# Attended sums from fp32r high and low parts, group parts by pairs of tiles, an update in 64x64 pieces

## The reference

```python
h = tok_ref(x)                      # embeddings, layer norm, 8 heads of 64: Q, V; erase and update of traces; V_ret @ W_out.T
h = h + attn_ref(layernorm(h))      # below
h = h + ffn_ref(layernorm(h))       # soft mixture of 64 experts, 16 slots each

def attn_ref(x):
    q, k, v = split(x @ W_qkv + b_qkv)
    gw = softmax(gelu(v @ W_gp))                     # 49 groups
    group_weight = gw @ gw.T
    attn = softmax((q @ k.T) * scale * group_weight)
    a = sigmoid(alpha)
    return (((1 - a) * attn + a * group_weight) @ v) @ W_proj + b_proj
```

## Time and profile before

| | before |
|---|---|
| median of 3 runs | 452.79 us (452.72 to 452.94) |
| profiled execution | 452.15 us, of which the traced span is 450.3 us |
| granted PE clock | 1.00 of full speed (2.4 GHz) in every slice |
| the chain that ended last | PE 73%, DMA 9%, DVE 7%, POOL 5% of the span |
| PE busy | 427.2 us (95%); DVE 294.2 (65%), ACT 229.5 (51%), POOL 138.8 (31%) |
| costliest group | L918, 256 instructions, 46.2 us |

### The profile page before, as it was taken

The page is one execution under the profiler, slowest core; times in us unless marked ns, Lnnn a source line. Parts: engine busy times, 40 slices in busy tenths (PEclk is TensorE's granted clock), DMA queues, the critical chain, the costliest instruction groups (busy, mean ns, idle before and its releaser), DMA issues.

```text
span 450.3 us, 8295 instructions
## 1 busy us (share of the span) xinstructions
PE 427.2 (95%) x3098; PEld 355.3 (79%) x3098; DVE 294.2 (65%) x755; ACT 229.5 (51%) x415; POOL 138.8 (31%) x233
## 2 busy tenths in 40 slices
PE   7899999999999999899999999999999799999995
PEld 5667757788888887788888888899965477787895
DVE  6689773885857577777775777767775253454464
ACT  5587734798624636643324557978864312112220
POOL 5875110673100019500002780013731421211310
PEclk9999999999999999999999999999999999999999
DMA  3226100301000000500000000006359999999404
GB/s 99 65 66 223 61 2 0 106 2 29 1 1 1 0 1 0 212 1 1 0 0 1 2 0 1 1 1 270 152 208 408 378 352 381 390 366 382 143 12 140
DMA packets 14231, 50.23 MB, mean 112 GB/s; under 512 B 3504, under 2 KB 8240, under 8 KB 9968
## 3 DMA queue, kind: packets, MB, share of 16 engines
q1 hardware_dynamic: 7584, 43.21, 25.7%
q0 software_dynamic: 2912, 3.96, 3.1%
q10 hardware_dynamic: 3696, 2.54, 1.8%
HBM read 46.53 MB, written 3.15 MB: 110 GB/s over the span
## 4 chain that ended last, share of the span: by engine, by line
PE 73%; DMA 9%; DVE 7%; POOL 5%; issue 2%; ACT 2%; SPq 0%; POOLq 0%; DVEq 0%
DMA w1r<-in_p_w 9%; PE ps L918 8%; PE ps L964 8%; PE ps L1120 7%; PE ps L1061 3%; PE ps L898 2%; PE ps L692 2%; PE ps L1090 2%; PE ps L1107 2%; PE ps L944 2%; PE ps L596 2%; PE ps L945 2%; PE ps L947 2%; PE ps L948 2%; PE ps L946 2%
## 5 line engine op out<-in xcount | busy, mean ns | idle before, releaser
L918 PE MATMUL ps<-pr,et 128*128 128x192 f32 x256 | 46.2, 331 | 1.7 <-DVE et L1777 1.2
L1120 PE MATMUL ps<-ys,ct 128*128 128x192 f32 x256 | 45.2, 330 | 1.4 <-DMA ys<-ys_dram 1.4
L1952 DVE TENSOR_TENSOR res<-ps,res 128x384 f32<-128x384 f32 x64 | 35.7, 558 | 14.9 <-PE ps L1120 10.4
L1120 PEld LDWEIGHTS ps<-ys,ct 128*128 128x128 f32 x256 | 41.2, 190 | 4.8 <-issue 2.7
L918 PEld LDWEIGHTS ps<-pr,et 128*128 128x128 f32 x256 | 41.2, 189 | 4.5 <-ACT et L1348 2.7
L584 POOL DMA_DIRECT2D ys<-ys_dram x32 | 19.6, 617 | 69.8 <-DMA ys_dram<-ysb 68.9
L1464 ACT ACTIVATE hs<-ps 128x384 f32<-128x384 f32 x16 | 7.8, 490 | 58.5 <-PE ps L1061 58.5
L500 POOL TENSOR_SCALAR ve<-mv 128x1 f32<-128x1 f32 x32 | 10.0, 312 | 75.1 <-DVE mv L1792 41.9
L1337 ACT ACTIVATE scs<-ps,pr 128x1024 f32<-128x1024 f32 x16 | 17.8, 1114 | 29.9 <-PE ps L866 29.9
L1341 ACT ACTIVATE zz<-zz,nmx 128x1024 f32<-128x1024 f32 x16 | 18.4, 1151 | 26.0 <-DVE nmx L1771 25.8
L1943 DVE COPY ysb<-ps 128x192 f32<-128x192 f32 x16 | 5.7, 357 | 39.4 <-PE ps L1090 39.4
(11 more groups left out here) (314 smaller groups left out, 1175.4 us busy)
## 6 DMA issues: line engine op xcount, KB each, us to landing
w1r<-in_p_w SPq DMA_DIRECT2D x16, 1152.0 KB, 19.7
w2r<-in_p_w SPq DMA_DIRECT2D x16, 1152.0 KB, 19.3
ys_dram<-ysb ACTq DMA_DIRECT2D x16, 96.0 KB, 8.7
ys<-ys_dram POOLq DMA_DIRECT2D x32, 48.0 KB, 7.2
phT<-in_p_phi SPq DMA_DIRECT2D x1, 1024.0 KB, 4.8
wT<-in_p_qkv SPq DMA_DIRECT2D x1, 774.0 KB
out<-res SPq DMA_DIRECT2D x3, 192.0 KB, 3.4
out<-res ACTq DMA_DIRECT2D x3, 192.0 KB, 3.8
```

Source lines behind the costliest of these rows:

```text
L918: last = mm(d[:, 0:D], et[:, k, :], pr[:, b * KT + k, 1:1 + D], start=(k == 0), stop=(k == KT - 1))
L1120: last = mm(bank(5 + q % 3)[:, h * D:(h + 1) * D], ct[:, u % 2, k + h, :], ys[:, t % YR, b, :], start=True, stop=True)
L1952: v.tensor_tensor(res[:, i:i + 2, :], bank(5 + q % 3)[:, 0:2 * D].rearrange("p (h d) -> p h d", h=2), res[:, i:i + 2, :], ALU.add).then_in ...
```

## The change

- `attend(i)` no longer multiplies plain fp32. The exponentials are turned as before, but ACT now copies both halves into `et` as fp32r, and DVE subtracts (PSUM bank minus `et`) into a new tile `etl`, half by half, each half behind ACT's. POOL splits the values once per batch into `V[b]`: 192 columns hi, 192 columns lo. PE makes 8 fp32r products of `et` with all 384 columns of `V`, then 8 of `etl` with the 192 hi columns. DVE's `finish` adds both column blocks with the weight `cn`.
- The group part leaves `attend`: `u_pair(p)` makes it for two tiles at once (4 fp32r products) into bank 7, behind `turn(s-1)` in odd steps, and DVE adds 384 columns in one operation (`u_add`). On DVE `weight` moves from before `turn` to behind `z_tile`.
- POOL runs `values_hi(0)` before the first clearing of `X1L`, `values_lo(0)` right behind it, `values_hi(1)` and `values_lo(1)` behind the second clearing.
- SP loads ring buffer 0 only after all attended sums (`o_filled` = 16), because `V1` lies there.
- The update makes eight 64x64 pieces (16 products, M = 64, N = 64), which ACT copies at once.
- In the front, `hi_parts(0)` comes one step earlier on ACT, `masked` moves ahead of `normalise`, four warming products on PE come one step earlier, and DVE's copy of `wpT`'s row and the `eyeP` scalings move from behind tile 13 to step 2.
- `scores` is split in two functions; the order of its instructions stays.

```diff
         scs = sb("scs", [P, S], where=late)
-        et = sb("et", [P, KT, P], where=late)
+        et = sb("et", [P, KT, P], F32R, late)
...
         phT = sb("phT", [P, 2, NS], where=params)
+        etl = sb("etl", [P, KT, P], F32R, params)
+        V = [sb("V0", [P, KT, 2 * D], F32R, params)]
...
         KV = XC + W2N
+        tables = ExitStack()
+        V.append(sb("V1", [P, KT, 2 * D], F32R, tables))
+        tables.close()
...
+        U_PAIRS = NT // 2
+        def u_sums_at(b):
+            return 2 * b + 1
+        def u_pair_at(p):
+            return 3 + p if p else 2
...
             return acc_bank(b, j).rearrange("p (t c) -> p t c", c=256)
+        def half_turned(t, half):
+            return t[:, half * (KT // 2):(half + 1) * (KT // 2), :].rearrange("p k c -> p (k c)")
...
             sp.wait_ge(m["bias_ready"], 1)
+            sp.wait_ge(m["o_filled"], NT)
...
             pool.wait_ge(m["half_ready"], 1)
+            def values_hi(b):
+                nc.gpsimd.tensor_copy(V[b][:, :, 0:D], pr[:, b * KT:(b + 1) * KT, 1:1 + D]).then_inc(m["v_split"], 1)
+            def values_lo(b):
+                if b:
+                    pool.wait_ge(m["v_split"], 2 * b + 1)
+                nc.gpsimd.tensor_tensor(V[b][:, :, D:2 * D], pr[:, b * KT:(b + 1) * KT, 1:1 + D],
+                                        V[b][:, :, 0:D].bitcast(F32), ALU.subtract).then_inc(m["v_split"], 1)
+            pool.wait_ge(m["pr_taken"], KT)
+            pool.wait_ge(m["h_filled"], NT)
+            pool.wait_ge(m["h_taken"], NT)
+            values_hi(0)
+            pool.wait_ge(m["v_split"], 1)
...
                 nc.gpsimd.memset(X1L[b][DB:P, 1, :].bitcast(F32), 0.0).then_inc(m["x1l_zeroed"], 1)
+                if b == 0:
+                    pool.wait_ge(m["x1l_zeroed"], 1)
+                    values_lo(0)
+                    pool.wait_ge(m["v_split"], 2)
...
             pool.wait_ge(m["ones_written"], 1)
+            pool.wait_ge(m["pr_taken"], NT)
+            values_hi(1)
+            values_lo(1)
...
                     tok_T(s - 1)
-                if s == 2:
+                if s == 1:
...
             pe.wait_ge(m["bs_ready"], 2)
-            for t in range(HP):
-                c = slice(t * P, (t + 1) * P)
-                mm(bank(5)[:, c], wvT[:, 0, c], bs[:, 0, c], start=True, stop=False)
-                last = mm(bank(5)[:, c], wvT[0:DB, 1, c], bs[0:DB, 1, c], start=False, stop=True)
+            for h in range(HEADS):
+                t, r = divmod(h, 2)
+                c = slice(h * DT, (h + 1) * DT)
+                d = bank(5)[r * DT:(r + 1) * DT, t * DT:(t + 1) * DT]
+                mm(d, wvT[:, 0, c], bs[:, 0, c], start=True, stop=False)
+                last = mm(d, wvT[0:DB, 1, c], bs[0:DB, 1, c], start=False, stop=True)
...
                 if b:
-                    pe.wait_ge(m["et_copied_v"] if r else m["et_copied_a"], 2 + r)
+                    pe.wait_ge(m["et_copied_v"], 6 if r else 3)
...
                 pe.wait_ge(m["qpl_taken"], 2 * QPS - 2 + b)
+                if b:
+                    pe.wait_ge(m["u_taken"], u_pair_at(0))
...
-            def scores(i, held):
+            def query_keys(i, held):
...
                 last.then_inc(m["s_filled"], 1)
-                if i == 0:
-                    for j in range(QPS + 2, 2 * QPS):
-                        query(j)
+            def group_scores(i, held):
+                b, k = divmod(i, KT)
+                n = slice(k * P, (k + 1) * P)
...
                 if i >= 1:
-                    pe.wait_ge(m["et_copied_a"], i)
-                    pe.wait_ge(m["et_copied_v"], i)
+                    pe.wait_ge(m["et_copied_v"], 2 * i)
...
                 b, k = divmod(i, KT)
-                n = slice(k * P, (k + 1) * P)
+                if k == 0:
+                    pe.wait_ge(m["v_split"], 2 * (b + 1))
...
                     pe.wait_ge(m["o_taken"], i - 1)
-                else:
-                    pe.wait_ge(m["u_taken"], i + 1)
+                if i == 0:
+                    pe.wait_ge(m["u_taken"], u_sums_at(0))
+                elif i == 1:
+                    pe.wait_ge(m["u_taken"], u_sums_at(1))
+                elif i % 2:
+                    pe.wait_ge(m["u_taken"], u_pair_at(i // 2))
                 d = bank(6 + i % 2)
-                mm(d[:, 256:256 + D], gD[b][:, n], uP[:, b, :], start=True, stop=False)
-                mm(d[:, 256:256 + D], gL[b][:, n], uP[:, b, :], start=False, stop=True)
-                for k in range(KT):
-                    if k == 0:
-                        pe.wait_ge(m["et_copied_a"], i + 1)
-                    if k == KT // 2:
-                        pe.wait_ge(m["et_copied_v"], i + 1)
-                    last = mm(d[:, 0:D], et[:, k, :], pr[:, b * KT + k, 1:1 + D], start=(k == 0), stop=(k == KT - 1))
+                for c in range(KT):
+                    if c % (KT // 2) == 0:
+                        pe.wait_ge(m["et_copied_a"], 2 * i + 1 + c // (KT // 2))
+                    mm(d[:, 0:2 * D], et[:, c, :], V[b][:, c, :], start=(c == 0), stop=False, skip_group_check=True)
+                for c in range(KT):
+                    if c % (KT // 2) == 0:
+                        pe.wait_ge(m["et_copied_v"], 2 * i + 1 + c // (KT // 2))
+                    last = mm(d[:, 0:D], etl[:, c, :], V[b][:, c, 0:D], start=False, stop=(c == KT - 1), skip_group_check=True)
                 last.then_inc(m["o_filled"], 1)
+            def u_pair(p):
+                pe.wait_ge(m["u_taken"], u_sums_at(1) if p else u_sums_at(0))
+                if p:
+                    pe.wait_ge(m["o_taken"], 2 * p)
+                for h in range(2):
+                    b, k = divmod(2 * p + h, KT)
+                    n = slice(k * P, (k + 1) * P)
+                    d = bank(7)[:, h * D:(h + 1) * D]
+                    mm(d, gD[b][:, n], uP[:, b, :], start=True, stop=False)
+                    last = mm(d, gL[b][:, n], uP[:, b, :], start=False, stop=True)
+                last.then_inc(m["u_filled"], 1)
...
                 if s < NT:
-                    scores(s, pass_tiles(s - 1))
+                    query_keys(s, pass_tiles(s - 1))
+                if s == 0:
+                    for j in range(QPS + 2, 2 * QPS):
+                        query(j)
+                if s < NT:
+                    group_scores(s, pass_tiles(s - 1))
...
                     turn(s - 1)
+                if s % 2:
+                    u_pair(s // 2)
...
             for s in range(NT + 3):
-                if 2 <= s < NT + 2:
+                if s == 1:
+                    hi_parts(0)
+                if 3 <= s < NT + 2:
                     hi_parts(s - 2)
+                if 2 <= s <= NT:
+                    masked(s - 2)
...
                     masked_q(s - 3)
-                if 2 <= s <= NT:
-                    masked(s - 2)
...
             act.wait_ge(m["update_done"], 1)
-            for r in range(2):
-                rows = slice(r * DT, (r + 1) * DT)
-                last = sc.copy(tt[rows, :, :], bank(5)[rows, :].rearrange("p (t c) -> p t c", t=HP)[:, :, r * DT:(r + 1) * DT])
-            last.then_inc(m["update_taken"], 1)
+            sc.copy(tt[:], bank(5)[:, 0:HP * DT].rearrange("p (t c) -> p t c", t=HP)).then_inc(m["update_taken"], 1)
...
                     act.wait_ge(m["in_phi"], 16 * 4)
-                    act.wait_ge(m["u_filled"], NB)
+                    act.wait_ge(m["u_filled"], u_sums_at(1))
...
             def turn(i):
-                act.wait_ge(m["et_filled"], 2 * i + 1)
...
                     act.wait_ge(m["o_filled"], i)
-                sc.copy(et[:, 0:KT // 2, :].rearrange("p k c -> p (k c)"), bank(4)).then_inc(m["et_copied_a"], 1)
+                for half in range(2):
+                    act.wait_ge(m["et_filled"], 2 * i + 1 + half)
+                    sc.copy(half_turned(et, half), bank(4 + half)).then_inc(m["et_copied_a"], 1)
...
                     lo_parts(s - 2)
+                if s == 2:
+                    v.tensor_copy(wpT[DB:DB + 1, 1, :], beta_row).then_inc(m["setup_taken"], 1)
+                    for r in range(2):
+                        rows = slice(r * DT, (r + 1) * DT)
+                        v.tensor_scalar(eyeP[rows, :], ident[rows, rows], TRACE_DECAY, None, ALU.mult)
...
                     wrap(0)
-                if s == NT + 1:
-                    v.tensor_copy(wpT[DB:DB + 1, 1, :], beta_row).then_inc(m["setup_taken"], 1)
-                    for r in range(2):
-                        rows = slice(r * DT, (r + 1) * DT)
-                        v.tensor_scalar(eyeP[rows, :], ident[rows, rows], TRACE_DECAY, None, ALU.mult)
...
                 d = bank(6 + b)[:, 0:D]
-                dve.wait_ge(m["u_filled"], b + 1)
+                dve.wait_ge(m["u_filled"], u_sums_at(b))
...
                                        ALU.subtract).then_inc(m["u_taken"], 1)
+            def u_add(p):
+                dve.wait_ge(m["u_filled"], u_pair_at(p))
```

(16 more changed lines are left out.)

2 lines of the change are left out of this document (1 added, 1 removed).

## The result

| | before | changed |
|---|---|---|
| median | 452.87 us (4 runs, 452.72 to 453.21) | 457.26 us (4 runs, 456.02 to 460.65) |
| ratio | | 1.0107, 95% interval 1.0086 to 1.0127 |
| profiled execution | 452.15 us, span 450.3 | 456.25 us, span 454.5 |
| mean granted clock of the 4 runs | 1.00 in the profiled one | 0.996, 0.988, 0.982, 0.990 |

The kernel became slower by 1.1%. The direction was the likeliest in the prediction, the size was not: 454.3 was forecast, with a range that ended at 456.8. And the runs now lie 4.6 us apart, the longest with the lowest clock.

The account below looks back on a forecast made before the run. PE, busy 95% at full clock, was taken as the bound, with POOL and DVE in its way in attention. Front -3.7, turns 0, collisions +3.3 and +1.9 gave +1.5 on 452.15: 453.65, median 454.3 (+0.64); range 449.3 to 456.8.

Parts of the forecast that it names:

- loop of the front: Front, PE-bound loop: with masked ahead, PE's waits for xm go and the loop starts earlier, -1.5 us.
- `cc`: Front: DVE's row copy and scalings leave the way of cc, for which PE waited 1.09; -1.0 us.
- update in pieces: Front: 16 products of 64x64 pieces take 2.1 us in place of 3.33; -1.2 us.
- first collision: Batch 0, before gw_T: POOL's values_lo(0) holds the shared port against DVE's L1667; PE +3.3 us.
- second collision: Before the first sum: values_lo(1) on POOL holds up DVE's small L1729, delaying uP; +1.9 us (0 to 2.5).
- group products ahead of tile 0's sum, four for two: Attention: 4 products of 0.11 in every second gap of 1.28 between transposes and sum, taken as free.
- turns, tile 0 to 15: Attention loop: new sums save PE 0.28 per turn, 4.5 over 16 turns, but DVE and ACT waits leave zero.
- Tile 1: Attention: its sum waited for uP and then two products, now only for uP; -0.3 us.
- Tiles 4 to 8: Attention, steps 5 to 8: DVE's side work delays remainders and ACT; +1.4 us, lag +1.1 at tile 8.
- Tile 15: Last attention turn: its transposes wait for exps, which comes 0.9 later within the turn; +0.7 us.
- the locks don't bite: Rival on POOL's splits: DVE wins the port or the small operation passes; 449.1 us, chance 0.26 shared with PE's gain whole.
- slower still: Rival in the attention loop: remainders come too late in every turn, 16 x 0.2 lost, 457.5 us; chance 0.10.

Follow-up runs that it names:

- e2: Changed kernel with POOL's values_lo(0) and values_lo(1) each waiting until DVE has written that batch's group weights; 452.67 us median, ratio 0.9996.
- e3: e2 with the update in four 128x128 blocks as in the kernel before; 450.01 us median, ratio 0.9936.
- e6: e5 plus twelve products nobody reads in PE's idle stretch ahead of the transposed group weights; 453.99 us, ratio 1.0025.
- e8: Kernel before with the reordered front alone, old update and old attended sums; 449.37 us median, ratio 0.9916.
- e5: Changed kernel with the old update in four 128x128 blocks, both POOL-DVE collisions left in; 455.53 us, ratio 1.0049.
- e1: Changed kernel with only POOL's values_lo(0) waiting for DVE's group weights of batch 0; 454.63 us median, ratio 1.0033.
- e13: e3 with DVE's side work spread, z_tile ahead of turn, and values_lo(1) also waiting for the bias tables' remainders; 444.44 us, ratio 0.9876.
- e7: Kernel before with the update in eight 64x64 pieces and ACT's single copy, nothing else; 453.98 us median, ratio 1.0028.
- e4: Changed kernel, collisions left in, plus twelve products nobody reads in PE's idle 3 us ahead of the transposed group weights; 458.22 us median.
- e9: e3 with DVE's side work (reduction, scalings, remainders) and ACT's two casts spread over other steps; 446.89 us, ratio 0.9915.
- e11: e3 with z_tile moved ahead of turn on DVE; 448.86 us, ratio 0.9957.
- e15: e2 with one 512-column fp32r product nobody reads behind each of the eight update pieces; 455.17 us median, ratio 1.0088.

## Why the prediction was wrong, step by step

The prediction's sum was +1.5 against the profiled execution; measured is +4.1 (456.25 against 452.15). Two steps carry the miss: the update, put at -1.2, and the clock, for which the sum has no term. Term by term:

| step | predicted | measured | from |
|---|---|---|---|
| loop of the front | -1.5 | -1.6 | 2.66 at L670 less the wait for `cc` |
| `cc` | -1.0 | -1.1 | the wait of 1.09 is gone |
| update in pieces | -1.2 | +0.45 | e2 against e3 |
| first collision | +3.3 | +2.84 | `gw_T` at 113.15 against 112.58 - 2.26 |
| second collision | +1.9 | +1.2 | e6 against e3 at tile 0, 4.04, less 2.84 |
| group products ahead of tile 0's sum, four for two | 0 | +0.2 | e3 against e8 at tile 0 |
| clock behind the stall | none | +1.4 | the rest at tile 0; 1.54 in e5 against e6 |
| turns, tile 0 to 15 | 0 | +0.5 | table |
| tile 15 to the end | 0 | +0.2 | span +4.2 |

**Right: both collisions.** Their place, their order and the operations they hit were as put down, and e1, e2 and e13 show that the operation is back at 0.57, 0.16 and 0.76 once the split stands elsewhere. The page SBUF — State Buffer of the Trainium skill (Who interferes with whom) says that issue order decides who blocks, and that a DVE instruction with two SBUF inputs collides with a GpSimd instruction that reads SBUF; the runs agree three times, down to an operation of a single column. The sizes were too high by 0.5 and 0.7: the split takes 3.18 and not 3.5, and the product of one column is held 2.04, where the prediction's own times give some 2.9 (122.55 to 125.5).

**Wrong: the update.** "between 16 x 0.08 ... and the same 3.3: I take 2.1". The bound itself failed. 3.3 stands as the worst case without a row for it; the pieces took more. Twice as many of half the size: 0.255 for one product of 64 columns (62.75 to 66.56, 15 distances), 0.42 for one of 128 (e3, eight in 3.34). The head products of 0.08 were the wrong row, though not by their type: they are plain fp32 too, 8 products in 16 instructions. What makes a piece three times as dear as a head product of 64 columns, no run shows.

**Wrong: "at the full clock" taken as given.** The sum treated PE's time as a property of its instructions. The change does two things to the clock: it makes PE idle for 2.98 (1.4 lost behind it in the changed kernel's profile, 2.7 in e5's, against e6), and it feeds it 3.8 us of narrow products (3.0 to 4.7 lost in the three profiled runs that show it, e7, e4 and e1, and 14 of 40 runs have a mean clock under 0.99). The price of a stall has to be taken with what the engine needs to come back. The page TensorE: Matmul & The Clock Gate of the Trainium skill (Loop structure matters more than you think) says that matmuls behind a long wait run at the lower clock; the trace agrees, with 0.42 for 0.23 at 115.22. The same page of the Trainium skill (Why this matters for your kernels) ties falls to gaps in which PE is idle, and the fall behind the pieces came with PE busy 4.00 of 4.00; there the measurement decides. The forecast of the median (profile + 0.64) was 0.4 short, since the median is 1.0 above the profiled run, which had no fall behind the pieces; that the other runs had one is likely by their clocks of 0.988 and 0.982, but not traced.

**Nearly right: the turns.** Predicted was that of PE's gain nothing arrives; measured is a loss of 0.5, and e3 against e8 repeats it without the rest. The parts:

- PE's gain per free turn is 0.15 to 0.25, 0.19 in the mean, not 0.28: the distances from tile 8 to 14 won 1.14 where 1.7 was put down. The sum is not what was mis-sized. It lasts 2.31 to 2.33 (2.30 predicted) and gives 0.34; but the gap between transposes and sum, taken as 1.28 in both kernels, is 1.42 now. The products with 384 columns follow each other at 0.180 to 0.185, taken was 0.175. The figure of the page TensorE: Matmul & The Clock Gate of the Trainium skill (Back-to-back issue gap), an estimate of 0.163 for 384 columns, is further off.
- Tile 1 -0.27 (predicted -0.3). The distances 1-2 and 2-3 lost 0.27 and 0.31: `gw_lo` stands ahead in step 3 as in step 4, PE waits 0.22 and 0.34 for it, and only step 4 was counted.
- Tiles 4 to 8: +0.9 (predicted +1.4), by the waits that were named, for `etl` in tiles 5 and 6, for ACT in tile 7, for `X2L` ahead of tile 8. e9 takes DVE's side work apart, and these turns shrink from 8.09 and 8.88 to 6.99 and 7.09.
- Tile 15: +0.62 (predicted +0.7), by the wait for `exps`; e11 moves `z_tile` up and the loss is gone (14-15 at 4.56).

**The rivals.** That the remainders are late in every turn is refuted: in tiles 9 to 14 PE never waits for `etl`. That the locks don't bite, likewise. The time that came, 457.3, is close to the figure of "slower still", 457.5, but not by its mechanism.

Three things stay open. Why a piece costs what it does. Why the profiled runs' low stretch behind the same stall was 1.4 long in effect once and 2.7 another time, and why the kernel before read 1.5 to 2 us less on two of the chips while the other kernels' times follow their traces from chip to chip. That the narrow products as such pull the clock down rests on e2, e3, e7 and the count of runs; e15, which was to show it from the other side, agrees with six runs only.

## What to carry to other kernels

Where POOL gets a long operation that reads SBUF, list the DVE operations with two SBUF operands that can start inside it, however small, and put it behind the last one on the path: here one wait on a semaphore was worth 2.8 us and its clock. Judge an edit of a matmul stream by the runs' spread and granted clock as well as by its columns: halving the work of a product saved nothing, and in some runs the fall behind the narrow stream cost up to ten times the 0.45 of the stream itself. An engine that gets faster is worth what the next one allows; here the saving on PE was worth nothing as ordered in the change, and spreading DVE's side work gave more (3.2 to 3.6 us by the start of tile 15's sum, with the old sums as with the new) than the whole rewriting.

## What the runs showed of the hardware that I had not expected

- PE's clock fell to 1.2 GHz with PE busy in every slice: at the end of or behind 3.8 us of plain fp32 products with 64 columns, for some 7 to 10 us; 4.6 to 4.7 us lost in e1 and e4, 3.0 in e7.
- Behind idle stretches of 2.98 (changed kernel), 2.97 (e5) and 3.18 (e15) PE ran at 1.2 GHz; in the place of the second, twelve products for nobody kept the clock up, and were worth 1.5 us (e6).
- An fp32r product of 512 columns costs 0.42 between plain fp32 ones, 0.23 among its like, both at a granted clock of 1.00 (e15).
- Plain fp32, cost of a product (two instructions with their weight loads): 0.255 with 64 columns and 0.42 with 128 in the update, 0.08 with 64 columns in the head products.
- POOL: 128x1536, fp32r remainder from two operands 3.18, cast 1.48.
